# Four value units moved from the end of one stage to the first slots of the next, in a two-layer attention and FFN kernel

## The reference, cut to what matters

```
v_img = (ctx @ vi_w + vi_b)            # 2048 x 512 by 512 x 2048, 16 heads of 128: the "value units"
k_img = rms_norm(ctx @ ki_w + ki_b)    # the same sizes: the "key units"
# first layer, for each head of width 32:
C  = (q @ k.T / sqrt(32)) * D          # D: the decay matrix, exp of a gate row minus its running maximum
h  = C / max(|sum C|, exp(-m)) @ v     # then a norm over the head's width
```

## Time and profile before

| what | us |
| --- | --- |
| median of 3 executions | 1513.53 |
| lowest and highest of them | 1510.12, 1520.15 |
| the profiled execution, its own time | 1518.07 |
| its span | 1516.4 |
| values stage, start of span to last value matmul | 257 |
| heads stage, first instruction to last key matmul | 260 to 561 |

### The profile page before, as it was taken

How to read it: one execution, slowest core, us unless ns; L and a number is a source line. 1 busy time by engine, 2 the same in 40 slices (tenths; PEclk the granted TensorE clock), 3 DMA queues, 4 the chain that set the end, 5 groups by cost and what they waited for, 6 DMA issues and landing times. The chain is left out here.

```text
span 1516.4 us, 25967 instructions
## 1 busy us (share of the span) xinstructions
PE 1376.7 (91%) x7406; PEld 1141.0 (75%) x7407; DVE 822.2 (54%) x1534; ACT 770.7 (51%) x1874; POOL 401.7 (26%) x375
## 2 busy tenths in 40 slices
PE   6899998999898977998998957999968999999979
PEld 5786666887777867877877635878867888888867
DVE  2442332367676785544444227734238877777845
ACT  4222223578686855215555543445438666656641
POOL 0110101327273810447933024211025300000041
PEclk9999999699999986999999987999978999999989
DMA  7998344897777820347564675663535555555312
GB/s 238 352 335 316 138 140 127 291 300 247 242 259 229 267 94 1 134 157 209 176 187 133 232 235 168 182 215 118 188 118 165 170 154 164 162 160 161 105 35 111
DMA packets 172053, 281.18 MB, mean 185 GB/s; under 512 B 29824, under 2 KB 64384, under 8 KB 171712
## 3 DMA queue, kind: packets, MB, share of 16 engines
q1 hardware_dynamic: 147120, 227.85, 47.4%
q0 software_dynamic: 7712, 26.22, 5.3%
q10 hardware_dynamic: 17136, 26.09, 4.7%
HBM read 173.40 MB, written 106.70 MB: 185 GB/s over the span
## 5 line engine op out<-in xcount | busy, mean ns | idle before, releaser
L2533 ACT ACTIVATE attend_prob<-banks,attend_row,rq 128x128 f32<-128x128 f32 x256 | 113.8, 455 | 53.0 <-DVE attend_row L2600 53.0
L100 PE MATMUL banks<-of_shared_split,heads_wl 128*128 (+1 forms) x256 | 109.6, 428 | 19.8 <-ACT heads_ksq L944 14.6
L100 PE MATMUL banks<-of_shared_split,of_ctx_lead 128*128 128x512 f32 x256 | 107.3, 419 | 9.4 <-DVE of_ctx_trail L419 5.6
L100 PE MATMUL banks<-of_x_lead,queries_wl 128*128 128x512 f32 x256 | 102.2, 399 | 4.2 <-ACT queries_sq L2183 2.7
L100 PE MATMUL banks<-attend_wol,attend_ol 128*128 (+1 forms) x256 | 105.8, 413 | 0.0
L102 PE MATMUL banks<-of_shared_split,of_ctx_trail 128*128 128x512 f32 x256 | 103.9, 406 | 0.0
L102 PE MATMUL banks<-of_shared_split,heads_wt 128*128 (+1 forms) x256 | 103.4, 404 | 0.0
L101 PE MATMUL banks<-of_shared_split,heads_wl 128*128 (+1 forms) x256 | 103.4, 404 | 0.0
L101 PE MATMUL banks<-of_shared_split,of_ctx_lead 128*128 128x512 f32 x256 | 103.0, 402 | 0.0
L101 PE MATMUL banks<-of_x_trail,queries_wl 128*128 128x512 f32 x256 | 100.8, 394 | 0.0
L102 PE MATMUL banks<-of_x_lead,queries_wt 128*128 128x512 f32 x256 | 100.7, 393 | 0.0
(11 more groups left out here) (339 smaller groups left out, 3618.0 us busy)
## 6 DMA issues: line engine op xcount, KB each, us to landing
mlstm_gmax<-running_max SPq DMA_DIRECT2D x36, 512.0 KB, 5.6
heads_raw<-in_L_xattn_ki_w SPq DMA_DIRECT2D x32, 512.0 KB, 6.0
k_heads<-heads_key ACTq DMA_DIRECT2D x64, 256.0 KB, 4.4
q_heads<-queries_head SPq DMA_DIRECT2D x64, 256.0 KB
attend_q<-q_heads SPq DMA_DIRECT2D x64, 256.0 KB
of_attend_k<-k_heads SPq DMA_DIRECT2D x60, 256.0 KB, 4.1
of_attend_v<-v_heads SPq DMA_DIRECT2D x60, 256.0 KB, 3.3
sorted_rows<-values_zeros SPq DMA_DIRECT2D x2, 5120.0 KB, 18.2
```

Source lines behind the costliest of these rows:

```text
L100: nc.tensor.matmul(out, lead_l, lead_r, start=first, stop=False)
L2533: ins = nc.scalar.activation(prob[:, j % 2, b, :], ps[:, j % 2, b * S:(b + 1) * S], ACT.Exp, bias=row[:, j % 2, 1, b:b + 1], scale=rq[:, b ...
```

## The change

Units u = 60 to 63 (quad 3, batches 12 to 15) are taken out of the values stage, whose loops now run to DONE = 60. They are formed in the heads stage by `held(v)`, v = 0 to 3, into banks 6 and 7, and DVE copies them into `A.out` (`keep_held`): v = 0 and 1 ahead of slot 0, v = 2 behind slot 1, v = 3 behind slot 3. Since `lead` and `trail` are gone by then, SP loads group 3's split context back from `split_dram` into `E1.split[:, 0]` at u = 52 of the values stage, 2 loads of 1 MB. For that the weights' halves are laid the other way round: quad q's two parts lie together in `E1.split[:, q % 2]`, so that half 0 is free once quad 2 is done. The key units' first split context goes to the same half 0, and so its eight loads move from the head of SP's list to slot 4, behind a wait for all four held units; the 1 MB store of the held values follows them, and only then the fourth load of context rows. The last store of the values stage is now one from `values_out`, on a semaphore that SP's final waits include.

```diff
         plain = xnT
-        wl, wt = E1.split[:, 0], E1.split[:, 1]
+        wl, wt = E1.split[:, :, 0], E1.split[:, :, 1]
+        DONE = UNITS - GB
         out = [sb("out", [P, 4, GB, DH1]), A.out]
...
-            for u in range(UNITS):
+            for u in range(DONE):
                 q, b = divmod(u, B)
...
                         sp.dma_start(A.ctx[:, b4, :], a["ctx_2048"][b4]).then_inc(A.loaded_ctx, 16)
+                if u == UNITS - B + 4:
+                    sp.wait_ge(product, UNITS - B)
+                    sp.wait_ge(split_stored, 2 * G * 16)
+                    for k in range(2):
+                        sp.dma_start(E1.split[:, 0, k].bitcast(F32),
+                                     split_dram[k, :, :, (G - 1) * N:].rearrange("c p t -> p c t")).then_inc(A.held_loaded, 16)
                 for g in range(G):
...
                             load_g(1)
-            k = UNITS // 4 - 1
+            k = DONE // 4 - 1
             sp.wait_ge(even_done, 2 * k + 2)
...
                          out[k % 2][:].rearrange("p h b e -> p h (b e)")).then_inc(stored[k % 2], 16)
-            sp.wait_ge(stored[0], 16 * UNITS // 8)
+            sp.wait_ge(stored[0], 16 * (DONE // 8 + 1))
             sp.wait_ge(split_stored, 2 * G * 16)
...
                 turn_plain(t)
-            for u in range(UNITS):
+            for u in range(DONE):
                 if u + C < G * C:
...
                 weight_trail(0, c)
-            for u in range(UNITS):
+            for u in range(DONE):
                 q, b = divmod(u, B)
...
                 turn(t)
-            for u in range(UNITS):
+            for u in range(DONE):
                 unit(u)
...
-def heads_and_keys(nc, K, M, A, E1, ctx_dram, ln_scale, xn_dram, ct_dram, g_dram, split_dram, w_dram, b_dram, k_dram, rk):
+def heads_and_keys(nc, K, M, A, E1, v_dram, ctx_dram, ln_scale, xn_dram, ct_dram, g_dram, split_dram, w_dram, b_dram, k_dram, rk):
...
         cut_lead, cut_trail = sem("cut_lead"), sem("cut_trail")
+        held_product, held_done = sem("held_product"), sem("held_done")
+        HELD_AT = {1: 2, 3: 3}
         EARLY = (G - 1) * GB
...
             load_raw(1)
-            for part in range(2 * C):
-                load_split(0, part)
             sp.dma_start(kbias[:], b_dram.rearrange("(h p) -> p h", p=P), allow_slow_non_contiguous=True
...
                         ph.hold(sp, held_sp)
+                    if n == 4 and first:
+                        sp.wait_ge(held_product, GB)
+                        for part in range(2 * C):
+                            load_split(0, part)
+                        sp.wait_ge(held_done, GB)
+                        sp.dma_start(v_dram[H1 - 4:, :, B - GB:, :].rearrange("h l b e -> l h (b e)"),
+                                     A.out[:].rearrange("p h b e -> p h (b e)")).then_inc(A.v_stored, 16)
                     if 1 <= n <= GB:
...
                     decayed(g, n + 1, first)
+                    if first and n in HELD_AT:
+                        keep_held(HELD_AT[n])
                     lagging(g, n - LAG + 1, weight_trail)
...
+            def keep_held(v):
+                dve.wait_ge(held_product, v + 1)
+                if v == 0:
+                    dve.wait_ge(A.v_stored, 16 * (H1 * B // 32 - 1))
+                nc.vector.tensor_copy(A.out[:, :, v, :], ps[:, 6 + v % 2, :].rearrange("p (h e) -> p h e", h=4)
+                                      ).then_inc(held_done, 1)
+
             decayed(0, 0, True)
+            keep_held(0)
+            keep_held(1)
             body(0, True)
...
+            def held(v):
+                if v == 0:
+                    pe.wait_ge(A.held_loaded, 32)
+                elif v >= 2:
+                    pe.wait_ge(held_done, v - 1)
+                rows = slice(v * S, (v + 1) * S)
+                for c in range(C):
+                    ins = three_passes(nc, ps[:, 6 + v % 2, :], split[:, 0, 0, c, rows], split[:, 0, 1, c, rows],
+                                       split[:, 1, 0, c, :], split[:, 1, 1, c, :], c == 0, c == C - 1)
+                ins.then_inc(held_product, 1)
+
             def keys(g, m):
                 u = unit_number(g, m)
+                if isinstance(u, int) and u == 0:
+                    pe.wait_ge(held_done, GB)
                 if m == 0:
...
                     outputs(g, n, first)
+                    if first and n in HELD_AT:
+                        held(HELD_AT[n])
             scores(0, 0, True)
+            held(0)
+            held(1)
             body(0, True)
...
         A.out = E1.raw[:, 0:4 * GB * DH1].rearrange("p (k b d) -> p k b d", k=4, b=GB)
-        A.v_stored = ph.sem("v_stored")
+        A.v_stored, A.held_loaded = ph.sem("v_stored"), ph.sem("held_loaded")
         A.loaded_ctx = ph.sem("loaded_ctx")
...
             values_and_gates(nc, K, M, A, E1, lead, trail, a, v_dram, split_dram, blank_dram, xn_dram, ct_dram, g_dram)
-        heads_and_keys(nc, K, M, A, E1, a["ctx_2048"], a["L0_xattn_ln_scale"], xn_dram, ct_dram, g_dram, split_dram,
+        heads_and_keys(nc, K, M, A, E1, v_dram, a["ctx_2048"], a["L0_xattn_ln_scale"], xn_dram, ct_dram, g_dram, split_dram,
                        a["L1_xattn_ki_w"], a["L1_xattn_ki_b"], k_dram, rk)
```

## The result

The changed kernel ran at a median of 1521.3 us (20 runs, 1514.2 to 1528.1), beside 1515.8 us for the kernel before, measured together with it (20 runs; 19 of them lie from 1509.5 to 1520.8, one took 3172.9 and does not count in the ratio). The ratio is 1.0033 with a 95% interval of 1.0017 to 1.0050, so the change costs 5.0 us (2.6 to 7.6). That is less than the 1% that was called "same", but more than nothing, and 1521.3 lies above the range of 1508 to 1519.5.

A forecast was written before the change was run, and what follows sets the result against it. PE, busy 91%, was taken as the bound, with idle time at the border of the stages. A start 7.2 us earlier and 7.2 us more up to the first key unit's end sum to 0.0: 1513.5 us, range 1508 to 1519.5.

The forecast's parts named there:

- "same": Whole time: a difference under about 1% (15 us), what a measurement can tell from no change; chance 0.95.
- Part 1: End of the values stage: 11.0 us taken out, 3.8 paid for the last store's landing, heads stage 7.2 us earlier.
- S: The heads stage's first instruction on SP, 259.72 in the profile before; forecast at 252.5, 7.2 us earlier.
- Part 2: Heads stage up to the first key unit's end: 36.7 us after S instead of 29.5, 7.2 us more.
- rival 2: Clock falls between held 2 and held 3: held 3 takes up to 5.2 us for 2.8, +2.4 us; chance 0.3.
- large case: Clock never rises before the held units are done: held 1 to 3, outputs and scores low, +11 us; chance 0.05.
- The landing: Last of the eight key loads before the first key unit: 4.3 us from issue at S + 27.0 to landing.
- Part 3: Context rows behind the eight loads: landing near S + 35, hidden by 1 us; 4 us later would lose 2 us.
- Rival 1: Full clock at the first key unit, 2.5 us sooner, or loads landing soon too, 1514.4 us; chance 0.2.
- Rival 3: The heads stage gets no earlier start, so all of Part 2 is added, +7 us; chance 0.03.
- The sum of the parts: At the first key unit's end: 7.2 us earlier start against 7.2 us more after S, sum 0.0.

The follow-up runs named there:

- e3: The changed kernel without the last four value units, the eight key loads back at the head of SP's list; ratio 0.9972 to the kernel before.
- e8: The changed kernel with the values stage's two output buffers swapped, so the stage does not wait for its last store's landing; ratio 0.9994 to the kernel before.
- e4: The changed kernel with eight added matmuls, result unread, two behind output 0, six behind output 1 and held 2; ratio 1.0016 to the kernel before.
- e1: The changed kernel with all four held units in one block behind the first scores, the eight loads still in slot 4; ratio 1.0013 to the kernel before.
- e6: e2 with four full-precision matmuls, result unread, in PE's waits at heads 3 to 5; ratio 0.9987 to the kernel before.
- e10: e4 with two context row loads and one maxima load moved from ahead of the eight key loads to behind them; run once, 1519.6 us.
- e9: e8 with e6's changes: swapped buffers, held units in one block, key loads in slot 2, four filler matmuls; ratio 0.9965 to the kernel before.
- e7: The kernel before with eleven filler matmuls, three behind the first scores and eight in the waits of heads 1 to 7; ratio 0.9997 to the kernel before.
- e2: e1 with the eight key loads moved from SP's slot 4 to the head of slot 2; ratio 0.9969 to the kernel before.
- e5: e4 with the 1 MB store of the held units moved to slot 12 on SP, behind the first key unit; ratio 1.0008 to the kernel before.

## Why the prediction was wrong

**Part 1 was right.** 7.2 us earlier was forecast, 7.4 measured, and e3 and e8 confirm its terms (3.8 for the landing: 3.6). The absolute times given with it (store near 247, stage from 252.5) were missed by some 1.5 us, because this execution reached unit 58 that much later. The loads at u = 52 cost nothing: held 0 started right behind the scores, at S + 2.2.

**Part 2 failed at one assumption: that the clock, once risen in held 0, stays up until held 3 is done.** The chain went as forecast up to held 2, which began at S + 12.2 (forecast 12.6). From there, against the forecast's own terms:

- held 2 took 4.4 us by its starts instead of 2.8, because the clock fell inside it: +1.6
- outputs 2 and 3 took 2.8, start to start, instead of 1.6: +1.2
- held 3 took 5.0 instead of 2.9: +2.1. It ended at S + 27.1, forecast 22.5: these three less the 0.4 by which held 2 began early, and 0.1 of rounding
- outputs 4 and 5 ran at full clock, but the scores and outputs 6 and 7 behind them at the low one (5.6 us for the 2.7 that they count for at full clock), so PE was ready at 290.5, S + 36.6, where I had said 28.7

That is the mechanism of rival 2, which I had priced at 2.4 us and given 0.3, with 0.05 for a large case. Its place was nearly right and its size was not: I let the clock fall once, behind 1.5 us of waiting, and it fell already within held 2, behind two outputs with a single wait of 0.57 us, again behind 1.47 us, and a third time behind 0.57 and 1.18 us. The rows had the warning: in the earlier trace rows it fell 0.8 us behind a wait of 1.38 us. I took it for a rival and built the sum on the case without it. e4 shows this most directly, since it *adds* matmuls, gets exactly the forecast end of held 3 (S + 22.4) and is 4.2 to 5.5 us sooner at the key unit; e1 (no waits between the held units, no fall) and e6 (fillers in front of the key unit, full clock in it) show the same from two other sides. That the first key unit itself would be at the low clock was forecast rightly.

**The landing was mis-sized too, and cost 1.0 to 1.3 us beside the clock.** I took 4.3 us for the last of eight and noted 9.2 as the far end. It took 7.3. On the path that ended last, that of the loads, the 6.6 us by which they were late are 4.6 for the end of held 3, 3.0 for the landing, and 1.0 less for the issues. In the changed kernel that hides behind the low clock but for 1.3 us (loads at S + 37.9, PE at S + 36.6), and in e4, where the clock is as I forecast, the unit ends at S + 37.7 for 36.7. The nearest row was the eight's own (6.9 to 9.2 in the earlier trace rows, and the 9.2 is the last one's); I preferred the quickest single load of 256 KB on the ground that little was ahead of them in the queue, and e10, which takes 1 MB from ahead, moved the end of the key unit by only 0.5 us. The Trainium skill's rule for one transfer ("DMA: Bandwidth & Descriptors", "Anatomy of one DMA"), by which the last load would land 2.6 us after its issue, does not hold here for the last of eight issued 0.46 us apart: 6.2 to 8.0 us were measured. The page fitted it on another issuing path. An issue itself took 0.46 us and not 0.62, so the eight left SP in 3.7 us instead of 5.0. Together, 6.5 us more than the forecast's 36.7: 5.2 for the clock (36.6 for the 31.4 at which the unit was to start), 1.3 for the loads.

**A row was misread.** I put the 7.97 us for which the first `mlstm_q` load is being issued down to the eight split loads ahead of it. They are gone from there, and it still takes 5.94 us (256.33), 4.80 in the second profile, and 4.5 to 6.8 in the ten profiles without them, beside 6.1 to 8.0 in the four with them. So most of that time is not theirs. The misreading cost the forecast nothing, since I had put that wait under the held units.

**Part 3 was right for the changed kernel.** POOL waited for the context rows, and ACT was not held up:

```profile
294.94 0.61 POOL L817 COPY heads_ctx<-mlstm_ctx 128x512 f32<-128x512 f32 x1 [23.41 <-DMA mlstm_ctx<-in_ctx]
```

```profile
298.00 1.27 ACT L906 ACTIVATE heads_dec<-mlstm_gmax,mlstm_nat 128x128 f32<-128x128 f32 x4
```

The rows landed at S + 40.8 and not near 35, but the key unit was later by as much. The copy stood some 3 us behind the start of the first key unit, and the exponential right behind that unit's end, as it did in the earlier trace rows. A wait of 23.41 us costs nothing here. The narrow margin that Part 3 named was real: in e3, e6, e9 and e10 it was used up, and the third key unit waited 1.2 to 2.1 us for its accumulator bank.

**Rival 1** (full clock at the first key unit) did not occur; its price of 2.5 us was about right, as e7 shows (2.8). **Rival 3** was rightly small.

**The sum of the parts.** Locally 13.7 us were added to S against 7.2 forecast, and S came 7.4 earlier: +6.3, in the second profile +5.2, in the time +5.0. The forecast of "within 1%" holds; the predicted number and its range do not. Of the 7.8 us between 1513.5 and 1521.3, 2.3 are not the change's: the median of three runs of before, on which I built, was 1513.5, that of twenty is 1515.8. The 5.5 that are left would have stayed just inside the range (1519.0), with the same step wrong. The range was drawn from the runs of before alone and from small rivals, and left out the case in which the low clock lasts through several units.

## What to carry to other kernels

Work moved into a stretch of short waits is not paid at its full-clock price: price each piece at the clock of that stretch, and ask of every wait ahead of it, short ones too, whether a row shows the clock falling after one like it. The same four units cost 5.8 us less in one block ahead of the waits (e1, read locally), and a gain over the kernel before was seen only when the loads that depend on the block were moved up as well (e2). And ask what stands behind the point that is moved up: here the context rows took some 2 of the 6 to 9 us back. Measure such a change at a landmark near it, counted from another landmark near it: here that repeats within 0.2 to 1.3 us, while the rest of the program alone differs by 7 us between executions.

## What the runs showed of the hardware

- Added matmuls made PE finish sooner. In e4 eight more brought the outputs behind the second scores from 3.02 to 1.97 us and held 3 from 5.0 to 2.8; in e7 the first key unit came down from 5.25 to 2.84 us. In the time of the whole program neither e4 nor e6 nor e7 shows a gain from them that is clear of noise.
- The same pause does not always end at the same clock. After 2.75 us without a matmul at the border the scores took 1.17 us in both profiles of the kernel before (and in e7, after 2.78), and 2.09 us in e8 and e9 (2.76). The pause and the instruction are the same, the unbroken run of value units ahead is not (six units before and in e7, two in e8 and e9); what decides was not found.
- Eight loads of 256 KB issued within 3.7 to 4.2 us need 9.6 to 11.3 us from the first issue to the last landing, with a 1 MB store right behind them or not (e5) and with 1 MB more or less ahead (e10). Other transfers were in flight in all of them (3.5 MB in all in e4 and e5), so what the eight need alone stays open.
- The clock is granted differently from execution to execution for the same instructions: 952.6 to 960.2 us for the last 4576 matmuls. The runs of one kernel spread over 11 to 14 us, and this is part of it: of the changed kernel's twenty, the longest (1528.1 us) had a mean granted clock of 0.933, the shortest (1514.2) one of 0.949.
- The `mlstm_q` load that SP issues right behind the 8 KB `kbias` load takes 4.5 to 8.0 us to be issued in all 14 profiles, with the eight split loads ahead or without; the later ones take 0.3 to 0.7. That the load ahead of it is the cause was not tested.

An own buffer for the held units' operands, with which the key operands could be loaded during the values stage, was not tried.
